# Own products inside the marks, ScalarE at every third quad, and a reordered SyncE queue in a four-layer graph network kernel

## The reference

```python
gathered = edge_weight[:, None] * x[edge_col]                        # edge_col = dst, edge_row = src of the call
neigh = segment_sum(gathered, edge_row, num_segments=3125)
out = x @ weight[:256] + neigh @ weight[256:] + bias
x = layernorm(x + out)
```

## Time and profile before

| | us |
|---|---|
| three runs | 3577.78, 3588.09, 3592.00 |
| median | 3588.09 |
| profiled execution, its own time | 3576.91 |
| its span | 3575.1 |
| TensorE matmul busy | 2961.2 (83%) |
| VectorE busy | 2435.7 (68%) |
| GpSimd busy | 1683.7 (47%) |
| ScalarE busy | 1527.0 (43%) |

### The profile page before, as it was taken

One profiled execution on the slowest core, in us unless ns is written; L12 is line 12 of the kernel. 1 busy time (PEld: TensorE's weight loads), 2 busy tenths in 40 slices (PEclk: granted clock), 3 DMA queues, 4 the chain that ended last, 5 costly groups with the idle time before them and its releaser, 6 DMA issues. The chain is left out here.

```text
span 3575.1 us, 59355 instructions
## 1 busy us (share of the span) xinstructions
PE 2961.2 (83%) x15273; PEld 1895.3 (53%) x15274; DVE 2435.7 (68%) x5480; ACT 1527.0 (43%) x3125; POOL 1683.7 (47%) x1731
## 2 busy tenths in 40 slices
PE   5789999989999598978769976776986569999996
PEld 2235444667777344467644434553443357587675
DVE  8895333568888898954789976569985763343444
ACT  1452222379998366631046655004654440310402
POOL 2777773046555766205777771576777300000000
PEclk6899999999999799978979997798998679999998
DMA  7998888378998365356721110993445233133241
GB/s 311 343 347 311 314 297 299 116 236 257 268 270 263 114 192 166 107 210 215 226 63 28 27 27 7 312 302 105 128 133 182 66 103 122 50 122 99 85 135 36
DMA packets 392781, 625.09 MB, mean 175 GB/s; under 512 B 129011, under 2 KB 274100, under 8 KB 385486
## 3 DMA queue, kind: packets, MB, share of 16 engines
q1 hardware_dynamic: 254085, 427.07, 36.4%
q0 software_dynamic: 72144, 145.54, 13.8%
q10 hardware_dynamic: 66365, 50.39, 4.3%
HBM read 442.67 MB, written 183.69 MB: 175 GB/s over the span
## 5 line engine op out<-in xcount | busy, mean ns | idle before, releaser
L1526 ACT ACTIVATE onehot<-iota,drel 128x128 f32<-128x128 f32 x1248 | 381.7, 388 | 684.8 <-PE ps L1231 345.1
L1231 PE MATMUL ps<-shared_sb,onehot 128*128 128x264 f32 (+1 forms) x1600 | 552.0, 441 | 93.2 <-DVE accum L2322 88.3
L2322 DVE TENSOR_TENSOR accum<-accum,ps 128x264 f32 (+1 forms) x1248 | 528.2, 423 | 10.6 <-DVE accum L2322 4.0
L1231 PEld LDWEIGHTS ps<-shared_sb,onehot 128*128 128x128 f32 x1600 | 259.4, 199 | 384.8 <-issue 239.6
L790 POOL DMA_INDIRECT t_w<-early_sb x391 | 379.6, 971 | 172.3 <-issue 94.0
L807 POOL TENSOR_SCALAR onehot<-iota,carry_d 98x512 bf16<-98x512 f32 x28 | 44.7, 1601 | 783.1 <-PE ps L1308 645.7
L1291 PE MATMUL ps<-counts_r,h_hi 128*128 128x512 f32 (+1 forms) x1050 | 322.1, 388 | 12.2 <-DVE h_lo L2584 12.2
L826 POOL DMA_INDIRECT shared_sb<-table,src_x x272 | 259.2, 953 | 115.1 <-issue 76.3
L1291 PE MATMUL ps<-counts_r,h_lo 128*128 128x512 f32 (+1 forms) x1050 | 313.0, 379 | 0.0
L826 POOL DMA_INDIRECT rows<-table,src_x x184 | 179.4, 975 | 176.5 <-DMA table<-score_sb 92.0
L873 POOL DMA_INDIRECT resid_sb<-table,src_x x224 | 211.6, 944 | 89.2 <-issue 57.7
(11 more groups left out here) (438 smaller groups left out, 6031.1 us busy)
## 6 DMA issues: line engine op xcount, KB each, us to landing
t_w<-onehot SPq DMA_DIRECT2D x13, 6400.0 KB
accum<-t_hot SPq DMA_DIRECT2D x208, 256.0 KB
shared_sb<-t_adj SPq DMA_DIRECT2D x53, 640.0 KB, 9.9
resid_sb<-t_w SPq DMA_DIRECT2D x13, 1664.0 KB
t_aside<-rows POOLq DMA_DIRECT2D x40, 512.0 KB
resid_sb<-t_w SPq DMA_DIRECT2D x13, 1536.0 KB
score_sb<-t_w SPq DMA_DIRECT2D x12, 1664.0 KB
shared_sb<-t_w SPq DMA_DIRECT2D x12, 1536.0 KB
```

What stands on the lines that cost most here:

```text
L1231: pe.matmul(ps[:, RING[(HU * h + u) % len(RING)], 0:w], onehot[:, h % 2 * HU + u, :], around[g][place(g, i, h)][:, u, 0:w], start=True, st ...
L1526: last = act.activation(onehot[:, h % 2 * HU + u, :], iota[:, 0:P], ACT.Abs, bias=drel[:, bass.ds(step + u, 1)], scale=-1.0)
L2322: dve.tensor_tensor(to, to, bank.unsqueeze(1), ALU.add).then_inc(step_acc, 1)
```

## The change

ScalarE takes every third quad instead of every fourth. Its wait for a free mark buffer moves from before the four Abs to before the Relu. The own product of tile t is issued on TensorE behind the marks of quad 44 + 2t, in bank 7, and its sum on VectorE two quads later; each product waits for the previous sum. The turned sums use bank 6 alone, so a turn waits for the sum of the batch before. Three kinds of buffers move (`key_parts`, `spread_v` with its zeros, `sum_rows`) so that the first half of pair 0 has its place free. On SP the wait for `adj_rows` goes; the wait for the landed rows and the 27 spreading DMAs leave the zeros and go behind the loads of pairs 0 to 9 (the wait behind pair 0, three DMAs behind each of pairs 1 to 9); and the first half of pair 0 is loaded behind a wait for `values`, with the waits for `quad_sum` and `w_summed` only before its second half.

```diff
-SHARE = 4
+SHARE = 3
+OWN_AT, OWN_LAG = 44, 2
...
-        key_parts = [over(f"key_part{m}", "shared_sb", 2176 + m * EB * P, [EB * P]) for m in range(2)]
+        key_parts = [over(f"key_part{m}", buf, at, [EB * P]) for m, (buf, at) in enumerate((("resid_sb", 4224), ("accum", 1024)))]
...
-        spread_v = [resid_sb[:, n * 2 * WIDE:(n + 1) * 2 * WIDE].bitcast(BF16) for n in range(2)]
-        sum_rows = [resid_sb[0:32, 1152 + n * 512:1152 + n * 512 + 512] for n in range(2)]
+        spread_v = [resid_sb[:, 2 * HALF_W + n * 2 * WIDE:2 * HALF_W + (n + 1) * 2 * WIDE].bitcast(BF16) for n in range(2)]
+        sum_rows = [flat_a[0:32, 6208:6720], flat_k[0:32, 5984:6496]]
...
+        own_turn = {OWN_AT + 2 * t: t for t in range(NT)}
...
-            sp.wait_ge(*count("adj_rows", 1))
...
-                sp.wait_ge(*count("rows_out", 64))
+
+            def low_rows_out(these):
+
                 by_steps = t_lo.rearrange("n (j r) e -> (n j) r e", j=QU)
-                for i in range(S // UN + 1):
+                for i in these:
...
-            sp.wait_ge(*count("quad_sum", QUADS))
-            sp.wait_ge(*count("w_summed", QUADS))
+            sp.wait_ge(*count("values", 1))
             for i in range(PAIRS):
                 for half in range(2):
+                    if i == 0 and half == 1:
+                        sp.wait_ge(*count("quad_sum", QUADS))
+                        sp.wait_ge(*count("w_summed", QUADS))
...
+                if i == 0:
+                    sp.wait_ge(*count("rows_out", 64))
+                if 1 <= i < 10:
+                    low_rows_out(range(3 * (i - 1), 3 * i))
...
             def sums_turned(n):
 
                 pe.wait_ge(*count("sum_rows", n + 1))
-                if n >= 2:
-                    pe.wait_ge(*count("w_summed", START[n - 1]))
+                if n >= 1:
+                    pe.wait_ge(*count("w_summed", START[n]))
                 for u in range(L0H):
-                    mm = pe.transpose(ps[:, 6 + n % 2, u * 32:u * 32 + 32], sum_rows[n % 2][:, u * P:(u + 1) * P], ident[0:32, 0:32])
+                    mm = pe.transpose(ps[:, 6, u * 32:u * 32 + 32], sum_rows[n % 2][:, u * P:(u + 1) * P], ident[0:32, 0:32])
...
+            def own_product(t):
+
+                if t == 0:
+                    pe.wait_ge(*count("ld_x", 16))
+                    pe.wait_ge(*count("ld_w0", 16))
+                else:
+                    pe.wait_ge(*count("own_sum", t))
+                for c in range(DC):
+                    mm = pe.matmul(ps[:, 7, 0:D], cols[:, c, t * P:(t + 1) * P], weights[:, c, 0:D], start=(c == 0), stop=(c == DC - 1))
+                mm.then_inc(done("own_mm"), 1)
...
                     if n > 0 and k == START[n]:
                         sums_turned(n - 1)
+                    if k in own_turn:
+                        own_product(own_turn[k])
...
                 act.wait_ge(*count("key_ps", k + 1))
                 if k >= SHARE:
-                    act.wait_ge(*count("quad_sum", slot_before(k) + 1))
                     act.wait_ge(*count("same_act", k // SHARE))
...
                 act.wait_ge(*count("key_used", L0H * (k // SHARE) + L0H))
+                if k >= SHARE:
+                    act.wait_ge(*count("quad_sum", slot_before(k) + 1))
...
+            def own_sum(t):
+
+                if t == 0:
+                    dve.wait_ge(*count("ld_rows", 16))
+                dve.wait_ge(*count("own_mm", t + 1))
+                dve.tensor_tensor(cols[:, :, t * P:(t + 1) * P], ps[:, 7, 0:D].rearrange("p (c n) -> p c n", c=DC),
+                                  row("L0_gnn_bias").rearrange("p (c n) -> p c n", c=DC), ALU.add).then_inc(done("own_sum"), 1)
...
+                    if k - OWN_LAG in own_turn:
+                        own_sum(own_turn[k - OWN_LAG])
```

More of the change, by code:

```diff
@@ L343, in build @@
                   by_layer("segs_done", 4, 4, 4), by_layer("lrelu", 1, 1, 1), by_layer("alpha_sub", 2, 2, 2), by_layer("exp", 3, 2, 2),
-                  by_layer("scores", 1, 1, 1), by_layer("ln", NG, NG, NC, NG), by_layer("gin_z", NC, NC, NC), by_layer("gin_h", NC, NC), by_layer("norm", NG, NG, NC, NG),
+                  by_layer("scores", 1, 1, 1), by_layer("ln", NG, NG, NC, NG), [("own_mm", NT)] + by_layer("gin_z", NC, NC, NC), [("own_sum", NT)] + by_layer("gin_h", NC, NC), by_layer("norm", NG, NG, NC, NG),
                   [(f"elu_neg{k}", NC) for k in (1, 2)], [(f"elu_exp{k}", NC) for k in (1, 2)], [(f"elu_x{k}", NC) for k in (1, 2)],
@@ L347, in build @@
                   [(f"{n}{k}", c) for k in (1, 2) for n, c in (("gat_in", NC), ("self_sub", 1), ("gat_out", NG))] + [("elu2", NC)],
-                  [("weighted1", 2), ("self_w1", 1), ("weighted2", 2), ("self_w2", 1)], [("diag_clear", 1), ("apart", S // QU), ("gaps", 3 * (S // HU))], [("x1_back", 16), ("x2_back", 16)], [("quad_sum", QUADS), ("own_mm", NT), ("adj_turned", BLOCKS * PAIRS)], [("same_act", QUADS // SHARE), ("adj_staged", BLOCKS * PAIRS)], [("w_summed", QUADS), ("own_sum", NT)], [("step_mask", EB), ("te", 1), ("adj_rows", 1), ("key_parts", 1), ("adj_ev", 1), ("keys", 2), ("pre", 1), ("attr_split", 1)], [("te_ps", 3), ("adj_tp", 1), ("steps_ps", 2), ("steps_ev", 1), ("early_one", 1)],
+                  [("weighted1", 2), ("self_w1", 1), ("weighted2", 2), ("self_w2", 1)], [("diag_clear", 1), ("apart", S // QU), ("gaps", 3 * (S // HU))], [("x1_back", 16), ("x2_back", 16)], [("quad_sum", QUADS), ("adj_turned", BLOCKS * PAIRS)], [("same_act", QUADS // SHARE), ("adj_staged", BLOCKS * PAIRS)], [("w_summed", QUADS)], [("step_mask", EB), ("te", 1), ("adj_rows", 1), ("key_parts", 1), ("adj_ev", 1), ("keys", 2), ("pre", 1), ("attr_split", 1)], [("te_ps", 3), ("adj_tp", 1), ("steps_ps", 2), ("steps_ev", 1), ("early_one", 1)],
                   [("p0_" + n, c) for n, c in parts], [("rest_" + n, c) for n, c in in_three],
@@ L763, in _ @@
             pool.memset(zeros, 0.0).then_inc(done("zeroed"), 1)
-            pool.memset(resid_sb[:, 0:4 * WIDE], 0.0).then_inc(done("zeroed"), 1)
+            pool.memset(resid_sb[:, 2 * HALF_W:2 * HALF_W + 4 * WIDE], 0.0).then_inc(done("zeroed"), 1)
             pool.wait_ge(*count("te", 1))
@@ L2047, in summed @@
                 dve.wait_ge(*count("sums_tp", n + 1))
-                by_quad = ps[:, 6 + n % 2, 0:L0H * 32].rearrange("p (u k v) -> p k u v", u=L0H, v=4)[:, 0:BATCHES[n]]
+                by_quad = ps[:, 6, 0:L0H * 32].rearrange("p (u k v) -> p k u v", u=L0H, v=4)[:, 0:BATCHES[n]]
                 of_quads = slice(L0H * now.start, L0H * now.stop)
@@ L2071, in _ @@
             all_rows = lambda v, w=D: v.unsqueeze(1).to_broadcast([P, NT, w])
[L2072 to L2076, removed]
             def spread(k, now):
```

## The result

The changed kernel takes 3559.60 us (median of six executions, 3556.02 to 3567.46), the kernel before 3582.84 (six, 3577.78 to 3592.00): a ratio of 0.9937, 95% interval [0.9924, 0.9949], 23 us less. The forecast was 3569 in 3555 to 3587. The profiled execution of after took 3567.23 (span 3565.4), at the high end of its six, that of before 3576.91, at the low end of its own. So the two profiles lie only 10 us apart, and the difference has to be read by stages.

A forecast was written before the change was run, and what follows sets the result against it. TensorE was taken to release the dense product's loads, not the scatters. TensorE 28 us early, held at pair 11 by the last scatter, less 1 in reserve, left 19 us: from the median 3588.09 to 3569, range 3555 to 3587.

The forecast's parts named there:

- 28 us early to its dense pace: Dense product: TensorE is at its pace as if started at 287.7, 28 us before 315.9.
- the scatters would take 9 of them back at pair 11: Pair 11 waits for the last scatter's landing at 582.6 and starts at 594.7; 19 of 28 us remain.
- pair 10's loads in by 566: Dense product: pair 10's loads, 6.4 MB in 17 us, are in by 566, so the last scatter lands after 4 us.
- before pairs 10 and 11: Sign of being right in the dense product: TensorE stands idle before pairs 10 and 11; 3 to 6 us reckoned.
- marks ending near 290: Rival at the marks: ending at 290 with own products inside gives the same time; counted within the forecast's 0.56.
- The stream of scatters: GpSimd: sums ready at 80.5 let the scatters run 3.8 us early, the last out at 578.6.
- The marks: Stage before the dense product: marks end at 281.3, with 3 us of waits at 284, instead of 290.6.
- Quad 17 goes near 114: Marks: quad 17 goes near 114, where quad 19 went at 119.39, some 5 to 6 us earlier.
- the later zeros move forward: SP's queue: without 7.8 us of hole and 12 us of low-row work, the last zero is reported near 263, not 303.0.
- The low rows: Behind loads of pairs 1 to 9, three each: 0.4 us a pair, 3.6 us in nine, and 1.9 us of SP.
- released by the scatters at 548.6: Dense product: TensorE asks for pair 10's load at 547.2, the scatters release it at 548.6; pair 10 starts near 561.
- late landing: Rival at pair 11: crowded scatters land after 22 us, leaving a gain of 4 us, 3584; chance 0.22.

The follow-up runs named there:

- hold_after: Changed kernel with one more wait: GpSimd holds its fifth scatter until the marks of 15 quads are made; 3570.42 us, ratio 0.9955.
- loads_spread: Changed kernel with ScalarE's six loads issued one or two at a time before several of its quads, not all before quad 17; 3560.41 us, ratio 0.9919.
- both_streams: Changed kernel with eight scatters instead of four before the third batch's wait and ScalarE's six loads issued apart; 3553.73 us, ratio 0.9903.
- queue_as_before: Changed kernel with the wait for sorted edges back before the zeros and the landed-rows wait and low rows back inside them; 3587.87 us, ratio 0.9999.
- early_scatters: Changed kernel with eight scatters instead of four issued before the wait for the third batch's sums; 3561.65 us, ratio 0.9925.
- after_again: The changed kernel measured once more, with nothing altered; 3563.12 us, ratio 0.9929 to the kernel before.
- zeros_wait: Changed kernel with SP waiting for the sorted edges (`adj_rows`) again before the zeros; 3569.59 us, ratio 0.9956.
- low_rows_in_zeros: Changed kernel with the wait for the landed rows and the 27 low rows back among the zeros; 3559.18 us, ratio 0.9922.
- own_behind: Changed kernel with the own products put back behind the marks, in banks 0 to 3; 3576.41 us, ratio 0.9968.

## Why the prediction was right, and where its steps were off

**The number held, and the mechanism as far as the dense product; at pair 11 it did not.** The prediction said that TensorE would come 28 us early to its dense pace and that the scatters would take 9 of them back at pair 11. Read in the same way, at the load of pair 1, TensorE came 21.1 us early (308.44 against 329.56); its product itself started 24.0 early, where 31 were forecast. It kept 19.2 of them at pair 11 (595.2 by the rule, where 594.7 was forecast; the stage gained 19.2 where 19.7, or 19 with a reserve, was). So 7 us were never there, because the marks ended late, and only 2 went at the end, most of them to pair 10's late second half and the slow clock behind it: from the load of pair 10 to that of pair 12 after took 59.18 us and before 56.50. The step that failed is the one that has pair 10's loads in by 566: the second half was in at 579.35. The idle TensorE "before pairs 10 and 11" was not seen; it stood still for 4.27 us inside pair 10.

**How much of it was luck.** The prediction had seen that marks ending near 290 would give the same time, since the scatters would still release pair 11's load, and they did release it. Their limit would have let pair 11 start near 592.3 (an estimate, from the 10.3 us of `hold_after` and `loads_spread`), TensorE came at 595.5: two paths that nearly tie gave the forecast's number, and the one that decided was not the one named. In `hold_after`, `loads_spread` and `both_streams`, where TensorE is early enough or the scatters late enough, it is the scatters that decide, so the path itself is real.

**The errors in it cancelled.** The stream of scatters ran 2.6 us early and not 3.8: its fifth went at 82.36 where 80.5 was reckoned (0.8 us of it shows in VectorE's first use of the gathered rows, at 33.89 for 33.08, beside the earlier zeros). The last one's issue was over at 579.82 (578.86 + 0.96), forecast 578.6, and the load left 2.2 us later, where 4 were taken: 582.05 for 582.6. Behind the load, 10.5 us were forecast to the start and 1.6 for a slow clock; 13.2 passed by the rule, because TensorE was still at pair 10.

**The marks** ended at 291.5, not 284. "Quad 17 goes near 114": it went at 117.61, since the six loads took 21.5 us to issue (91.6 to 113.1), more than the 17.9 of idle time from which I reasoned. The other 4 us are in the pace: TensorE was busy for 50.92 of 53 us, and eight quads with four own products took 17.2 to 18.4 us, where 8 x 1.62 + 0.4 + 4 x 0.86 = 16.8 was reckoned; a product inside costs 1.13 us, not 0.86. What I left unasked is what the loads cost in all: `loads_spread` won 14.8 us at the end of the marks, beside the 24.0 of the change.

**The queue's part** was told as "the later zeros move forward" and given no price. `queue_as_before` gives it one: without it the whole gain is gone. The chain of the dense product's start had two ends of equal length, and the prediction followed one of them.

**The low rows** were put at 0.4 us a pair and 1.9 us of SP. SP needed 7.64 us for three, and TensorE nothing that shows: from the load of pair 1 to that of pair 10 it took 549.86 - 308.44 = 241.4 us, before 571.67 - 329.56 = 242.1. The cold start of the dense product cost 308.44 - 291.85 less 329.56 - 315.86, 2.9 us (3.3 forecast); the granted clock stood at 0.50, 1.2 GHz, from 290 to 295. SP's 7.64 us stood behind a load and had 12 us to spend.

**Pair 10** was said to be released by the scatters at 548.6; TensorE released it, at 549.86. Here I misread the code, in the description of the kernel before as well. A scatter waits for the one 8 places before it (`2 * NACC`, with `NACC = 4`), not 16. With 8, pair 10's quads are reported 31 places before the end, in after at 537.6, and the scatter that made GpSimd wait near 577 had landed after some 12 us, not 22. The rival "late landing" with 22 us rested on that number; with 12 it would have given 578.6 + 12 + 10.5 = 601.1, a gain of 13 us. Its mechanism is not refuted: `early_scatters` shows a landing of up to 10.9 us. The Trainium skill, "DMA: Bandwidth & Descriptors", section "Queues, rings and completion order", has the engines turn to another queue after each packet. The loads that left 2.3 to 3.6 us after the last scatter in four kernels agree with it; the 4.2 to 6.0 us of `after_again`, `zeros_wait` and `low_rows_in_zeros`, the 12 us and the 10.9 us beside a late load do not.

**From the stage to the total.** Behind the stage the code is the same in all fourteen profiles. From the first write of `t_hot` in layer 1 (739.04 before, 719.92 after) to the end of the profiled execution's own time they take 2837 to 2851 us, with no order by kind of kernel: before took 2837.9, nearly the least, after 2847.3. That is how 19.2 us of the stage became 9.7 in this pair of profiles. The medians differ by 23, 4 more than the stage. It may be that a typical execution of before loses more in the stage than its profiled one did: the four kernels without a gain read 696.9 to 706.6 there, at equal totals. No run shows it, as each of these has one profile.

## What to carry to other kernels

Where two streams end within a microsecond or two at the same place, as the zeros and the own products did at pair 0, and the scatters and a late load at pair 11, an experiment that takes away one of them can show nothing; test them alone and together before calling either free. A change that frees the busiest engine ends where the next stream stands, so work out that stream's own end first, with the depth of its waits read from the constants in the code. Then look at the row where the engine starts: a load that was released late holds nothing up if the engine comes later still. And look at where DMAs are issued as well as at what they move: issuing six loads apart moved the end of the marks by 14.8 us here, more than the 9.9 that shifting quads to the engine that issues them was worth.

## What was not expected of the hardware

**Issuing behind full queues.** With zeros in flight, the loads of x transposed and of x took 6.03 and 8.40 us to issue one after the other, and 0.39 and 0.37 us where each stood alone between two quads, with the same zeros running. SP's three DMAs of low rows, one behind the other, took 7.64 us. So the time to issue went with what the same queue had just been given, and not with the others' traffic alone; through what, no run shows.

**A slow stretch of the DMA engines.** In after, the DMA engines moved 1.44 MB in 571.5 to 582, mean 137 GB/s, with the second half of pair 10 outstanding until 579.35 and scatters besides. In 11.5 us of the stage before that, 544.5 to 556, they moved 3.81 MB:

```profile
DMA packets 1900, 1.44 MB, mean 137 GB/s; under 512 B 319, under 2 KB 1851, under 8 KB 1851
...
DMA packets 3649, 3.81 MB, mean 332 GB/s; under 512 B 1906, under 2 KB 3442, under 8 KB 3442
```

The first row is of 571.5 to 582. Such a stretch made one half-pair late in most versions (16.8 us to its use in before, 16.7 in after, 17.2 in `early_scatters`), near the last scatters, and there GpSimd waited for one of them (2.38 us in after, 2.67 in before, 4.28 in `low_rows_in_zeros`). In `loads_spread` and `both_streams`, where pair 10 was loaded before 570, it had no load to hold up. It is what came last at pair 11 in after. Its cause is open: no run here separates it from the scatters, the counts that ScalarE writes out, or the rows being read.

**The clock after a pause.** The idle of 4.27 us was followed by a granted clock of 0.54 (580 to 585), and one of 3.45 us in `own_behind` by 0.50 (581.4 to 584), the lower level, 1.2 GHz. After the one of 3.01 us in before it stayed at 1.00, from 588.4 to 597. The Trainium skill, "TensorE: Matmul & The Clock Gate", section "HAM oscillation — how this bites in real kernels", lets a product that pauses for its loads, some 3 to 5 us each time, restart cold each time: the traces of after and `own_behind` agree with it, and before, at the short end of that, kept its clock.
